# A two-layer macaron network on one core: the order around three kinds of hand-over between engines

## What is computed

```
x = x + 0.5 * ffn0(layernorm(x))        # silu(gate)*up, rms norm over 1024, ternary weights
x = x + attention(layernorm(x))         # 16 heads of 128, rotary embedding, softmax
x = x + 0.5 * ffn0(layernorm(x))        # the same weights again
x = x + 0.5 * moe(layernorm(x))         # 8 experts, best 2 of 8, and a shared expert
x = x + retention(layernorm(x))         # (Q K^T * decay) V, no softmax
x = x + 0.5 * moe(layernorm(x))
```

## Time and profile before

| | us |
|---|---|
| median of three runs (1627.71 to 1629.47) | 1627.77 |
| the profiled execution | 1626.63 |
| its span, first to last instruction | 1624.8 |
| PE busy | 1560.0 (96%) |
| DVE busy | 1242.3 (76%) |
| ACT busy | 1215.5 (75%) |
| POOL busy | 1169.5 (72%) |

### The profile page before, as it was taken

The page is one execution under the profiler, slowest core; times in us unless marked ns, Lnnn a source line. Parts: engine busy times, 40 slices in busy tenths (PEclk is TensorE's granted clock), DMA queues, the critical chain, the costliest instruction groups (busy, mean ns, idle before and its releaser), DMA issues. The chain is left out here.

```text
span 1624.8 us, 26806 instructions
## 1 busy us (share of the span) xinstructions
PE 1560.0 (96%) x9214; PEld 906.5 (56%) x9214; DVE 1242.3 (76%) x2324; ACT 1215.5 (75%) x1904; POOL 1169.5 (72%) x823
## 2 busy tenths in 40 slices
PE   3998899999999999999999999999999999999798
PEld 2565445555555555555555555555567556678575
DVE  7888787777777777777777777778878877987527
ACT  7876988988989988998888998888655643443442
POOL 0865888888888888888898888887575322567435
PEclk9999999999999999999999999999999999999999
DMA  9311878989779888879889789888202520000423
GB/s 308 127 53 44 139 143 163 152 144 182 152 143 180 152 151 172 151 150 168 154 153 169 149 145 156 158 140 145 53 1 59 130 55 1 1 1 24 105 82 97
DMA packets 641371, 197.10 MB, mean 121 GB/s; under 512 B 601547, under 2 KB 639062, under 8 KB 640982
## 3 DMA queue, kind: packets, MB, share of 16 engines
q1 hardware_dynamic: 636662, 188.19, 59.8%
q0 software_dynamic: 1536, 4.20, 0.8%
q10 hardware_dynamic: 3040, 3.02, 0.6%
HBM read 36.71 MB, written 10.22 MB: 29 GB/s over the span
## 5 line engine op out<-in xcount | busy, mean ns | idle before, releaser
L969 POOL TENSOR_TENSOR Pl<-Pm,Ph 128x1024 f16<-128x1024 f32 x256 | 546.0, 2133 | 44.6 <-ACT Ph L1310 44.3
L1300 ACT ACTIVATE Pm<-banks,nbias,s_scale 128x1024 f32<-128x1024 f32 x256 | 307.9, 1203 | 95.3 <-DVE nbias L1935 94.6
L1933 DVE TENSOR_REDUCE nmax<-banks 128x1 f32<-128x1024 f32 x256 | 311.8, 1218 | 87.4 <-PE banks L2501 87.0
L1310 ACT ACTIVATE Ph<-Pm 128x1024 f16<-128x1024 f32 x256 | 268.4, 1049 | 1.5
L948 POOL TENSOR_TENSOR rp_b<-rp_s,rope 128x512 f32<-128x512 f32 x128 | 163.0, 1274 | 97.7 <-ACT rp_s L1277 96.4
L1966 DVE SCALAR_TENSOR_TENSOR X<-banks,rinv,X 128x256 f32<-128x256 f32 x256 | 112.2, 478 | 112.8 <-PE banks L2501 112.8
L2499 PE MATMUL banks<-QK_hi 128*128 128x512 f16 x512 | 194.1, 379 | 1.6 <-DVE QK_lo L2024 0.9
L2499 PE MATMUL banks<-PT_hi,V_hi 128*128 128x512 f16 x512 | 194.0, 379 | 0.4 <-DMA PT_lo<-Pl 0.4
L2501 PE MATMUL banks<-QK_hi,QK_lo 128*128 128x512 f16 x512 | 194.0, 379 | 0.0
L2500 PE MATMUL banks<-QK_lo,QK_hi 128*128 128x512 f16 x512 | 194.0, 379 | 0.0
L2500 PE MATMUL banks<-PT_lo,V_hi 128*128 128x512 f16 x512 | 194.0, 379 | 0.0
(11 more groups left out here) (317 smaller groups left out, 3965.5 us busy)
## 6 DMA issues: line engine op xcount, KB each, us to landing
moe_raw<-in_L_ffn_W SPq DMA_DIRECT2D x48, 128.0 KB, 2.5
w_all<-in_L_attn_w_qkv SPq DMA_DIRECT2D x3, 2048.0 KB, 15.8
a_raw<-in_L_attn_w_qkv SPq DMA_DIRECT2D x24, 256.0 KB, 3.2
PT_hi<-Ph SPq DMA_TRANSPOSE x256, 3.4
PT_lo<-Pl SPq DMA_TRANSPOSE x256, 3.3
xs<-zeros SPq DMA_DIRECT2D x1, 2944.0 KB, 16.7
yd<-y_sb ACTq DMA_DIRECT2D x5, 512.0 KB, 2.9
raw_gu<-in_L_ffn_w_gate_up SPq DMA_DIRECT2D x2, 1024.0 KB, 7.3
```

What stands on the lines that cost most here:

```text
L969: nc.gpsimd.tensor_tensor(Pl[:, z % 4, :], Pm[:, k, :], Ph[:, z % 4, :], ALU.subtract).then_inc(pl_done.sem, 1)
L1300: nc.scalar.activation(Pm[:, k, :], two_banks[z % 2][:], ACT.Exp, bias=nbias[:, z:z + 1], scale=s_scale[:], accum_out=rsum[:, z:z + 1]).th ...
L1310: nc.scalar.activation(Ph[:, z % 4, :], Pm[:, (base * SLOTS + z) % 3, :], copy).then_inc(ph_done.sem, 1)
L1933: nc.vector.tensor_reduce(nmax[:, z:z + 1], two_banks[z % 2][:], AX, ALU.max, negate=True).then_inc(max_done.sem, 1)
```

## The change

In both networks, at `ht` = 2, PE makes the first down product ahead of `squares`; DVE makes `ln_normalise` ahead of `mean_squares`; POOL makes `rsqrt_rms` behind the low part and the sum of squares of the step. At the end of the second network `squares` stands behind the second down product; in the first it stays behind the first.

In the retention with `b` = 0, ACT's `normalise` of the first half moves from step 6 to step 5, its `ln_hi` from step 8 to 6, `normalise` of the second half is at step 7 and its `ln_hi` behind the loop as before. The first half's transposes use banks 4 and 5 in place of 6 and 7 and wait for two `add`s in place of four; the second half's use 6 and 7. DVE's second `shifts` stands behind the fourth `add`, its `ln_lo` of the first half at step 7. PE's wait for the second half's low part moves from ahead of the four last mixes to the third of them.

At the end POOL's `rows_lower` of the second half moves from behind step 8 to behind step 11, and `last_experts` does scatter of tile 0, root, scatter of tile 1, a new wait for the seventh `add` of the retention, scatter of tile 2, root, scatter of tile 3.

```diff
-    ROWS_LO_AT, BEST_AFTER, SECOND_AFTER, POSITIONS_AFTER = (2, 8), 3, 8, 11
+    ROWS_LO_AT, BEST_AFTER, SECOND_AFTER, POSITIONS_AFTER = (2, 11), 3, 8, 11
...
@@ POOL, ffn
                             rsqrt_ln(0, l + 1, 1)
-                        rsqrt_rms(phase - 1)
...
                     if ht:
                         sum_squares(s)
+                    if phase and ht == SQUARES_AFTER:
+                        rsqrt_rms(phase - 1)
@@ POOL, last_experts
-                scatter(range(2))
+                scatter((0,))
                 rsqrt_ln(1, l, 0)
-                scatter(range(2, 4))
+                scatter((1,))
+                pool.wait_ge(x_added.sem, x_added.at(1, RET_X + TT - 1))
+                scatter((2,))
                 rsqrt_ln(1, l, 1)
+                scatter((3,))
@@ ACT, retention
-                    if b == 0 and i in (SCORES_FIRST, SCORES_FIRST + 1):
-                        normalise(of_x, l_next, i - SCORES_FIRST)
-                    if b == 0 and i == SCORES_LN:
-                        ln_hi(of_x, l_next, 0)
+                    if b == 0 and i == SCORES_FIRST - 1:
+                        normalise(of_x, l_next, 0)
+                    if b == 0 and i == SCORES_FIRST:
+                        ln_hi(of_x, l_next, 0, 4)
+                    if b == 0 and i == SCORES_FIRST + 1:
+                        normalise(of_x, l_next, 1)
...
-                    ln_hi(of_x, l_next, 1, 4)
+                    ln_hi(of_x, l_next, 1)
@@ DVE, ffn
                         if ht == SQUARES_AFTER:
-                            mean_squares(phase - 1)
                             if phase < 3:
                                 ln_normalise(1, l, phase - 1)
                             else:
                                 ln_normalise(0, l + 1, 1)
+                            mean_squares(phase - 1)
@@ DVE, retention
                             add(t)
-                            if b == 0 and t == 2:
-                                shifts(of_x, l_next, 1)
-                    if b == 0 and i == SCORES_LN:
-                        ln_lo(of_x, l_next, 0)
+                        if b == 0:
+                            shifts(of_x, l_next, 1)
+                    if b == 0 and i == SCORES_LN - 1:
+                        ln_lo(of_x, l_next, 0, 4)
...
-                    ln_lo(of_x, l_next, 1, 4)
+                    ln_lo(of_x, l_next, 1)
@@ PE, ffn
+                    if phase and ht in AFTER_UP:
+                        down(phase - 1, AFTER_UP[ht])
                     if phase and ht == SQUARES_AFTER:
                         squares(phase - 1)
-                    if phase and ht in AFTER_UP:
-                        down(phase - 1, AFTER_UP[ht])
...
-                down(len(PHASES) - 1, 0)
-                squares(len(PHASES) - 1)
-                for j in range(1, TPH):
+                for j in range(TPH):
                     if f and j == 1:
                         pe.wait_ge(h_ready.sem, h_ready.in_head(f, NS))
                     down(len(PHASES) - 1, j)
+                    if j == f:
+                        squares(len(PHASES) - 1)
@@ PE, retention
                     elif t == TPH + 2:
-                        pe.wait_ge(x_added.sem, x_added.at(b, RET_X + t - 3))
+                        if b == 0:
+                            x_ready(of_x, l_next, 1)
+                        else:
+                            pe.wait_ge(x_added.sem, x_added.at(b, RET_X + t - 3))
...
                 if b == 0:
-                    pe.wait_ge(x_added.sem, x_added.at(b, RET_X + TPH))
-                    transpose_x(of_x, l_next, 0)
+                    pe.wait_ge(x_added.sem, x_added.at(b, RET_X + 2))
+                    transpose_x(of_x, l_next, 0, 4)
                 for i in range(SCORES_LN, N_SCORES):
                     scores(i)
                 if b == 0:
-                    transpose_x(of_x, l_next, 1, 4)
+                    pe.wait_ge(x_added.sem, x_added.at(b, RET_X + TPH))
+                    transpose_x(of_x, l_next, 1)
                     rotation(b + 1, (0, 1))
-                    x_ready(of_x, l_next, 1)
```

## The result

| | before | after |
|---|---|---|
| median, us | 1627.77 (1627.71 to 1629.47) | 1635.67 (1634.65 to 1637.74) |
| profiled execution, us | 1626.63 | 1636.1 |
| its span, us | 1624.8 | 1633.1 |
| mean granted clock | 0.994 | 0.990 |

After over before is 1.0048, 95% interval [1.0034, 1.0062]: slower by 7.9 us. Both medians are of five executions. The forecast was 1632.8. Lines of the parts behind the edits are six higher than before: `squares` L2589, `down` L2616, `ms` L1795, `XN` on DVE L1622, `transpose_x` L2515.

A forecast was written before the change was run, and what follows sets the result against it. PE was taken to bound the kernel, busy for 96% of the span. Networks +7.0, clock +2.4, retention -2.0 and last experts -2.4 gave +5.0 us, a median of 1632.8 us; range 1623.5 to 1636.

The forecast's parts named there:

- slower still: Rival: in retention the later copy of step 5 delays the rotation, holes only move; +7.0 us, 1634.8 us, chance 0.13.
- The sums no longer hold PE up: Networks: the first down product covers PE's waits for the sums of squares, at most 3.5 us won.
- First and second boundary: First network, first two steps ht == 2: PE's second down product waits for the mean, 3.4 and 3.5 us lost.
- First boundary of the second network: At 1177.27: nothing lost, or 0.9 us if one POOL operation falls on the normalisation; 0.4 us taken.
- The clock: Behind the two large stalls the granted clock may fall, 0 to 2.3 us each; 1.2 each taken, +2.4 us.
- The price of a POOL operation: Each large POOL operation beside DVE's four normalisation instructions costs 1.0 us; upper bound its full 1.3 us.
- The later root is hidden: First network: POOL's root comes 2.5 us later, but its user, the first add, stands two up products later.
- End of the second network: Squares behind the second down product close the hole of 1.18 us and the experts start earlier: -1.2 us.
- Retention: First half of the batch: both PE holes, 1.03 and 0.85 us, close; -2.0 us, bounds -2.1 and 0.
- Last experts: Earlier ranks and two fewer scatters ahead of the second root: -2.4 us, bounds -2.9 and -1.2.
- Mean soon enough: Rival: PE finds the mean made and all 3.5 us of the networks' holes are won; 1619.9 us, chance 0.15.
- Short stalls: Rival: fewer POOL operations fall on the normalisation and the clock stays; -0.8 us, 1627.0 us, chance 0.30.

The follow-up runs named there:

- e1: The changed kernel with DVE's mean_squares back ahead of ln_normalise in both networks: 1618.48 us, ratio 0.9947 to the kernel before.
- e6: The changed kernel with all network hunks undone, leaving the retention and last-experts parts: 1623.65 us, ratio 0.9975 to the kernel before.
- e3: The changed kernel with POOL's rsqrt_rms back in its old place: 1625.9 us, ratio 0.9987 to the kernel before.
- e9: The kernel before with only DVE's mean_squares moved behind ln_normalise: 1630.32 us, ratio 1.0017.
- e4: The changed kernel with 16 unused matmuls ahead of the second down product at the first network's first two boundaries: 1631.52 us, ratio 1.0025 to the kernel before.
- e2: e1 with POOL's rsqrt_rms also back in its old place: 1619.62 us, ratio 0.9949 to the kernel before.
- e7: The kernel before with the retention part alone (ACT, DVE and PE): 1625.95 us, ratio 0.9988.
- e8: The kernel before with the last-experts part alone (rows_lower at step 11 and the new scatter order): 1624.58 us, ratio 0.9979.
- e10: The kernel before with the new order of scatters and roots alone, rows_lower staying at step 8: 1625.2 us, ratio 0.9985.
- e11: The kernel before with rows_lower at step 11 alone, scatters and roots as before: 1628.7 us, ratio 1.0004.
- e12: e1 with the first network's last sums of squares also put behind the second down product: 1619.0 us, ratio 0.9947 to the kernel before.

## Why the prediction was right, and where it was off

The sign and the mechanism held; the time was 2.9 us over the forecast and inside the range. That it lies inside says little: the range ran from 1623.5, faster than before, to 1636, and the measured time is 0.3 us under its upper end. The rival with the nearest number, slower still (1634.8), has its mechanism refuted: the retention's holes closed. What speaks for the prediction is that the waits that it named stand where it put them. Point by point:

- **The sums no longer hold PE up.** Right: four of five waits gone. By itself, without DVE's order, this is a gain: e1 lies 5.2 us under e6, which has both networks as before (4.6 by the ratios, 0.9947 and 0.9975). I had 3.5 in the rival that wins all the holes. The traces show that this is not the same 3.5: e1 is 3.1 us ahead of e6 by the second network, where the holes are won, and nothing by the first two boundaries, where other waits took their place; the rest, 1.1 ahead of the second network and 1.1 behind the last transposes, is mostly slow stretches that e6 has (132.7 to 136.1 and 1504.9 to 1508.3) and e1 hasn't.
- **First and second boundary.** Right in size (3.1 and 3.5 against 3.4 and 3.5), and right in cause: PE waits for `ms`, `ms` for the four instructions, and these run beside two POOL operations. e1, e3 and e9 each take away one link, and the stall shrinks or goes.
- **First boundary of the second network, the term most off.** 1.8 for the stall against 0.4, with 1.5 more for the clock that I had not put there (1197.71 - 1190.72 = 7.0 us to the next transpose, 1184.37 - 1178.89 = 5.5 before). I had weighed none or one POOL operation; there were two again (`lo` at 1187.91, the sum at 1189.14), and the four took 3.27 us. What I had read in the trace of before, POOL's `lo` only at 1179.02, was late because it waited for ACT's high part, as its bracket says:

```profile
1179.02 1.29 POOL L899 TENSOR_TENSOR hT_lo<-ff_h,hT_hi 128x512 fp32r<-128x512 f32 x1 [0.66 <-ACT hT_hi L1201]
```

  ACT makes that part from an up product, and the change takes the hole of 0.79 us and a few tenths more out of PE's way to it: the up product started 0.5 us ahead of the normalisation before (1176.75, 1177.27) and starts 1.7 us ahead of it now (1185.66, 1187.32). So `lo` is ready sooner, and the root, which held it off in e3 (to 1183.76), no longer does. I had used both effects at the first boundary and neither here.
- **The clock.** Right in kind, too small in sum: 1.5 + 2.5 + 1.5 = 5.5 against 2.4. My bound of 2.3 for one stretch was passed at the second boundary. e4's two stretches are 1.6 and 2.6 shorter than the changed kernel's (7.0 and 8.0 us against 5.5 and 5.4), which is about the ledger's 1.5 and 2.5.
- **The price of a POOL operation.** The 1.0 us of the earlier trace rows held at every boundary where a large operation fell on the four. The upper bound that I had beside it, POOL's full 1.3 us lost each time, was misread: by the single rows at e2 the held instruction's own 0.4 us lie inside the hold.
- **The later root is hidden.** True for its own user, and beside the point: what mattered is what it held back on POOL. I had used this once, for the first boundary; the price of the whole edit, 9.8 us (e3), stood nowhere in the prediction as a term of its own.
- **End of the second network.** -1.2 forecast. The ledger has +0.6 for four things, of which 1.5 are clock, 0.3 and 0.4 the two boundaries: 0.6 - 2.2 = -1.6 for the end.
- **Retention.** -2.0, ledger -1.9, e7 -2.0. Both holes closed; the rival in which the rotation gets late is refuted.
- **Last experts.** -2.4, ledger -2.2, e8 -3.4 and e10 -2.4. That the earlier ranks would gain nothing of their own was right (e11). The hole ahead of the last transposes is 5.06 us, as I had it (3.6 and the 1.4 of the ranks); but another 1.37 stand in the hole before it, and the slow stretch behind the ranks, 0.66 in before, is gone.
- **Rivals.** "Mean soon enough" (1619.9) did not happen, but e1 is near to it, made by moving one call: 1618.5. Its gain in the networks, 3.8, is the size that I had, in other places (see e1). "Short stalls" (1627.0) is what e3 shows, 1625.9, with the guard back.

Attention returned 0.7 us of the delay, which no term had. In the ledger the sum came out low because the clock was 3.1 too small and the stall of the second network 1.4, while the end of that network, attention and the first stall gave 1.4 back.

## What to carry to other kernels

When a consumer on PE waits for a tiny operation, look at everything that stands ahead of it on its engine and at what a third engine runs at that moment: here 0.15 us of work, put behind 1.4 us of work, cost PE up to 4.3 us, since two POOL operations stretched the 1.4 to 3.3. An idle wait on an engine can be a guard; before moving the waiting instruction, ask which operations behind it will then start, and beside whom. Test the parts of a mixed change alone: this one held 9 us of gain, hidden under 17 us of loss that one moved call takes away. And compare times by several executions and not by one trace, as slow stretches of the clock come and go between executions of the same work.

## What the runs showed of the hardware that was not expected

- **The length of a hole does not tell whether the clock falls.** It fell behind 3.96 us and 4.30 (changed kernel) and 2.42 us (e3, second boundary), but not behind 2.03 (e3, first boundary). In the kernel before it fell behind the hole of only 1.78 us at the ranks. And behind one hole, that ahead of the last transposes, it stayed at 1.00 in e1 (3.37 us) and stood at 0.56 in e12 (3.36 us); the rows are at e12. The rows of e3 and then of before:

```profile
65.00:70.00 5.00, 4.98 (x30) 3.37 (x31) 1.57 (x3) 2.07 (x6) 3.65 (x4) 1.00 1.00 320
90.80:95.00 4.20, 4.14 (x19) 3.42 (x20) 0.51 (x1) 0.00 (x0) 3.47 (x3) 0.59 0.00 0
```

```profile
1486.00:1491.00 5.00, 4.21 (x31) 4.24 (x32) 4.62 (x15) 1.03 (x3) 2.74 (x4) 0.66 0.00 0
```

- At the end of the first network a hole of 0.88 us leaves the clock alone before, while behind 0.89 us in e2 it fell to 0.5 (2.4 to 1.2 GHz). This is not the order's doing: e6, e7, e8, e10 and e11 have the first network of before, instruction for instruction, and the clock fell there in the traces of e6 and e7 and not in those of the others. One execution of the same work has the stretch, another hasn't. With the hole closed (e12) it stayed at 1.00, which one trace can't put down to the closing. The rows are the same 5.5 us of e2, of e7 and of e12:

```profile
131.50:137.00 5.50, 5.50 (x35) 5.50 (x35) 3.32 (x15) 1.69 (x3) 2.00 (x2) 0.69 0.00 0
```

```profile
131.50:137.00 5.50, 5.43 (x33) 5.46 (x34) 3.50 (x14) 2.83 (x5) 1.89 (x2) 0.69 0.08 27
```

```profile
131.50:137.00 5.50, 5.50 (x49) 5.45 (x48) 3.35 (x15) 2.60 (x4) 2.00 (x2) 1.00 0.01 5
```

- So e2, 0.9 us ahead of e1 at the transpose of the second boundary (92.85 against 93.74), is 0.7 behind it at the start of attention (138.65 against 137.97). Differences of one or two microseconds between the traces of two versions of this kernel can be such a stretch and nothing else.
- Matmuls that nobody needs, put into two holes of 4 us, kept the clock at 1.00 and made the stretches behind them 1.6 and 2.6 us shorter (e4). The whole kernel was 4.1 us faster, of which the trace has 0.8 left at the last transposes.
- A POOL operation on four columns takes 1.0 to 1.2 us and leaves DVE's `TENSOR_SCALAR` alone; one on 512 columns takes 1.3 us and holds one `TENSOR_SCALAR` of 0.4 us until 0.15 us behind its own end, which costs 1.0.
